# Self loops of the neighbour counts: eight 4-column matmuls a strip in place of four of 392 columns

## The chip, the cores and the metric

The kernel runs as one program on one core of one Trainium2 chip. The metric is device time in microseconds (us); the kernel before takes 3985.91 us, the median of three runs (3983.66 to 3988.76). All lower times are better. The profiles are each of one execution, taken by the hardware profiler.

## The reference, cut to what matters

The network takes 6250 nodes with 128 features and 200,000 edges sorted by destination, runs one graph attention layer (10 heads of 13 features) and then four graph convolutions with self loops. In short:

```python
ft = (hn @ W_att).reshape(n, 10, 13)
scores = einsum('ehd,ehd->eh', ft[src], ft[dst]) / sqrt(13)
ex = exp(scores - segment_max(scores, dst)[dst])
agg = segment_sum(ft[src] * (ex / segment_sum(ex, dst)[dst])[:, :, None], dst)
...                                   # elu, projection, feed-forward on the nodes
# each of the four convolutions, with the same edges:
s = concatenate([src, arange(n)]); d = concatenate([dst, arange(n)])   # the self loops
deg = segment_sum(ones, d); dis = rsqrt(deg)
out = segment_sum((x @ W)[s] * (dis[s] * dis[d])[:, None], d) + b
```

A convolution is thus a product with the matrix A + I, whose entry (source, destination) counts edges, plus 1 on the diagonal. The kernel writes this matrix of counts to memory once, in bf16, and the four convolutions read it back as a moving operand.

## The kernel before, in words

The program goes through stages with a barrier between them: `prelude` (0 to 116 us), `attention` (116 to 2107 us), `normalise`, `general_attention`, `node_update`, and `convolutions` (from about 2360 us to the end). The change lies in `attention` alone.

`attention` is written out in full for NG = 196 groups of 1024 edges (GC = 8 columns of 128), and no loop is left in the program. Beside group k's edges, each step k also makes the counts of strip k: 32 destination nodes (SUB) against all sources. These are 6272 sources as 128 partitions by 49 tiles (NT). The strip is cut in four quarters q of two sets (QS = 2) of four destinations (HALF); a quarter is 2 x 196 columns in a PSUM tile `adj_ps`, of which there are two, taken in turn. A column of a quarter is (destination set a, source tile, destination within the set).

For each quarter, VectorE makes one-hot rows of the keys `ohk` (`key_one_hots`, L937), VectorE and ScalarE make the one-hot rows of the source's low part `ohl` (L932, L1030 and L1037), and TensorE adds up their products in `count` (L1133: four matmuls of 196 columns). Ahead of these, the matmul of L1129 puts the self loops in: the stationary operand is a 32 x 128 slice of `own_low`, the moving one a 32 x 392 window of `own`, a tile of zeros with ones at the strip's own source tile. It opens the accumulation (`start=True`) for all 392 columns. ScalarE then copies the quarter out as bf16 (`copy_quarter`, L1082), and after the fourth quarter the strip goes to memory (L1110).

The attention part of a step is a pipeline of lag LAG = 3: POOL gathers the sources' features with eight indirect DMAs a group (L900) into one of six buffers `fts`. TensorE spreads the destinations' features (`ftd_ps`, L1155), VectorE multiplies both and sums to scores (L951, L987, L992), ScalarE takes exponentials (L1061, L1068), VectorE weights the features (`terms`, L974), and TensorE sums them into `agg_ps` (L1189, L1207 to L1213).

The order on each engine is written out by hand in its `body(k)`. What couples the engines: POOL's first gather of group n waits for `terms` of group n - 6, and its fifth for the shift (L1057) of group n - 4. A quarter waits on TensorE for its keys and for ScalarE's copy of the quarter two before. VectorE's `first_products` waits for all eight gathers of its group.

Of the kernel before, what the change touches and what calls it, by code (L numbers as in the profile page):

```python
# [6 lines left out]
BF16 = mybir.dt.bfloat16  # L7
# [6 lines left out]
P = 128  # L14
# [18 lines left out]
SUB = 32  # L33
NS = NP // SUB
HALF = 4
NA = SUB // HALF
NH = NP // HALF
SC = 2
SW = SC * P
STRIP = NT * SUB  # L40
KEYS = NT * HALF
# [31 lines left out]
def gnn_program(nc, t):  # L73
# [16 lines left out]
    with top:  # L90
# [47 lines left out]
        with ExitStack() as lists:  # L138
            g["src_all"] = sb("src_all", [P, NG, GC], I32, lists)
            g["sched"] = sb("sched", [1, NG // UN, 2 * UN], I32, lists)  # L140
            g["key_cols"] = sb("key_cols", [P, NG, NA, SC], F32, lists)
            g["low_cols"] = sb("low_cols", [P, NG, NA, SC], F32, lists)
            g["shared"] = sb("shared", [WD, NG], F32, lists)
            g["spots"] = sb("spots", [5, P], FP16, lists)
            prelude(nc, t, sb, pb, sem, g, ln_batch)
            stage_over()
            attention(nc, t, sb, pb, sem, g)
            stage_over()
# [594 lines left out]
def attention(nc, t, sb, pb, sem, g):  # L743

    ft_tab, row_tab, agg_tab, adj, sched, src_all, shared, ident, ident_bf, spots, key_cols, low_cols = (g[k] for k in (
        "ft_tab", "row_tab", "agg_tab", "adj", "sched", "src_all", "shared", "ident", "ident_bf", "spots", "key_cols",
        "low_cols"))
# [8 lines left out]
    QS = 2  # L756
# [4 lines left out]
    with ExitStack() as c:  # L761
# [13 lines left out]
        terms = sb("terms", [P, 2, GC, WA], F32, c)  # L775
        res = sb("res", [WD, UN, WA], F32, c)
        iota_sb = sb("iota_sb", [P, KEYS + P], F32, c)
        own = sb("own", [SUB, NA, 2 * KEYS], BF16, c)
        own_low = sb("own_low", [SUB, 2 * P - SUB], BF16, c)
        lo_iota = sb("lo_iota", [P, P], FP16, c)  # L780
        ohk = sb("ohk", [P, 2, NA * SC, KEYS], BF16, c)
        ohl = sb("ohl", [P, 2, NA * SC, P], BF16, c)
# [3 lines left out]
        adj_ps = [pb(f"adj_ps{q}", [P, 512], F32, c) for q in range(2)]  # L786
# [7 lines left out]
        own_made = sem("own_made")  # L794
# [39 lines left out]
        def _(sp):  # L834
# [23 lines left out]
            for j in range(NG // UN):  # L858
                _, base = nc.values_load_multi_w_load_instructions(
                    sched[:, j, :], engines=[mybir.EngineType.SP], min_val=0, max_val=NP,  # L860
                    skip_runtime_bounds_check_because="node numbers, at most NP")
                for u in range(UN):
                    n = j * UN + u
                    if u % 2 == 0:
                        if j:
                            sp.wait_ge(close_done, n - UN + 2)
                        sp.dma_start(rows[0:4, u:u + 2, :], row_tab[n:n + 2].rearrange("g r e -> r g e")
                                     ).then_inc(rows_in[u // 2], 16)
                    if n >= UN:
                        sp.wait_ge(ftd_done, 4 * (n - UN) + 4)  # L870
                    sp.dma_start(win[:, u, :], ft_tab[ds(base[u], WD), :].unsqueeze(0).to_broadcast([2, WD, HD])
                                 ).then_inc(win_in[u], 16)
                    if n >= BACK:
                        store(n - BACK, base[UN + u])
                    if n == WEIGHTS_AT:
                        node_weights()
# [28 lines left out]
        def _(dve):  # L905
# [2 lines left out]
            nc.vector.memset(signs[:, 1:2], RS).then_inc(consts, 1)  # L908
            nc.vector.memset(rows[:], 1.0).then_inc(consts, 1)
            nc.vector.memset(fade[:], 1.0).then_inc(consts, 1)  # L910
            nc.vector.memset(own[:], 0.0).then_inc(own_made, 1)
            nc.vector.memset(own_low[:], 0.0).then_inc(own_made, 1)
            nc.vector.memset(hr_3[:], 0.0).then_inc(rest_zero, 1)
            dve.wait_ge(own_made, 2)
            nc.vector.tensor_copy(own[:, :, KEYS:KEYS + HALF], ident_bf[0:SUB, 0:SUB].rearrange("p (a d) -> p a d", d=HALF)
                                  ).then_inc(own_made, 1)
            nc.vector.tensor_copy(own_low[:, P - SUB:P], ident_bf[0:SUB, 0:SUB]).then_inc(own_made, 1)
            for s in range(2):
                nc.vector.memset(terms[:, s, :, WA - 1:WA], 1.0).then_inc(consts, 1)
# [200 lines left out]
        def _(pe):  # L1120
            def count(k, q):

                pe.wait_ge(keys_done, 4 * k.n + q + 1)
                if q * QC <= LD < (q + 1) * QC:
                    pe.wait_ge(ohl_done, k.n + 1)
                if q >= 2 or k.after(1):
                    pe.wait_ge(strip_done, 4 * k.n + q - 1)
                tile_of = own[:, q * QS:(q + 1) * QS, KEYS - HALF * k.j:2 * KEYS - HALF * k.j]
                nc.tensor.matmul(adj_ps[q % 2][:, 0:QS * KEYS], own_low[:, P - SUB - SUB * k.u:2 * P - SUB - SUB * k.u], tile_of, start=True, stop=False)  # L1129
                for a in range(QS):  # L1130
                    for m in range(SC):
                        n = q * QC + a * SC + m
                        last = nc.tensor.matmul(adj_ps[q % 2][:, a * KEYS:(a + 1) * KEYS], ohl[:, k.s, n, :],  # L1133
                                                ohk[:, k.s, n, :], start=False, stop=(a == QS - 1 and m == SC - 1))
                last.then_inc(adj_done, 1)

            def nearness(k):

                pe.wait_ge(rows_in[k.u // 2], 16 * (k.j + 1))
                if k.after(1):  # L1140
                    pe.wait_ge(oh_done, k.n)
                nc.tensor.matmul(near_ps[:], spots[:], rows[:, k.u, :], start=True, stop=True).then_inc(near_done, 1)
# [73 lines left out]
            def body(k):  # L1216
                nxt, one, two, late = k.at(1), k.at(-1), k.at(-2), k.at(-LAG)
                if late.exists():
                    broadcast_highest(late)
                if two.exists():  # L1220
                    turn_highest(two)
                if k.exists():
                    count(k, 0)
                if nxt.exists():
                    nearness(nxt)
                if k.exists():
                    count(k, 1)
                    count(k, 2)
                if one.exists():
                    last_features(one)  # L1230
                if nxt.exists():
                    closeness(nxt)
                if k.exists():
                    count(k, 3)
                if late.exists():
                    first_sums(late)
                    later_sums(late)
                if k.exists():
                    first_features(k)
                if late.exists():  # L1240
                    if late.after(1):
                        carried(late)
                    last_sum(late)
            zero = Group(0)
            pe.wait_ge(own_made, 4)
            nearness(zero)
            closeness(zero)
            steps(body, LAG)
# [1044 lines left out]
```

## Time and profile before

| | |
|---|---|
| median of 3 runs | 3985.91 us (3983.66 to 3988.76) |
| span of the profiled execution, first to last instruction | 3987.6 us |
| attention stage, first gather to last sum copied out | 117.3 to 2103.9 us |
| convolutions | about 2360 to 3987 us |
| busy over the span | PE 92%, PEld 54%, DVE 54%, ACT 47%, POOL 38% |

No own time apart from the span is given for the profiled execution; the span is taken for it, and it is 1.7 us above the median, inside the spread of the three runs. PE is TensorE's matmuls and PEld its weight loads, which overlap them; DVE is VectorE, ACT ScalarE, POOL GpSimd. Busy time is the time with an instruction recorded; for POOL's indirect DMAs that is the issue alone, and the data land later. The idle time before an instruction is given with what ended it, "issue" being idle time in which the engine waited for nothing that the profile shows. TensorE's clock has two levels here, 1.2 and 2.4 GHz, shown as 0.5 and 1.0; a mean between them is a mixture in time.

### The profile page before, as it was taken

How to read it: one execution, taken by the hardware profiler on the slowest of the kernel's cores; microseconds unless marked ns; L12 is line 12 of the kernel's file. 1: busy time of each engine (PE TensorE's matmuls, PEld its weight loads, DVE VectorE, ACT ScalarE, POOL GpSimd, SP SyncE). 2: the span in 40 equal slices, each digit the busy share in tenths (PEclk: the TensorE clock that was granted, in tenths of full speed). 3: DMA queues.
4: the chain of work that ended last, by engine and by line, in shares of the span. 5: the costliest groups of instructions: out<-in, count | busy, mean ns of one | idle time of the engine just before them, and what ended most of it. 6: DMA issues, size and time to landing. Idle time of an engine off the chain costs nothing. (4 is left out here: it accounts for less than half of the span.)

```text
span 3987.6 us, 61840 instructions
## 1 busy us (share of the span) xinstructions
PE 3679.6 (92%) x21902; PEld 2157.9 (54%) x21902; DVE 2167.3 (54%) x3396; ACT 1880.8 (47%) x5147; POOL 1505.2 (38%) x1605
## 2 busy tenths in 40 slices
PE   5899999999999999999985879999999999999999
PEld 3566666666666666666653544445444544454444
DVE  8788888888888888888874750002100210012000
ACT  4788888888888888888863660002000100011000
POOL 2677777777777777777760000000000000000000
PEclk8788888888888888888886989999999999999999
DMA  6443333333333333333334126665666566665665
GB/s 202 128 109 104 105 106 105 105 106 105 106 105 105 106 106 106 105 106 105 105 92 88 38 65 204 204 196 181 199 194 208 174 194 203 205 189 184 213 204 159
DMA packets 467250, 560.45 MB, mean 141 GB/s; under 512 B 45449, under 2 KB 411684, under 8 KB 466686
## 3 DMA queue, kind: packets, MB, share of 16 engines
q1 hardware_dynamic: 383558, 366.63, 30.4%
q0 software_dynamic: 51168, 107.68, 12.2%
q10 hardware_dynamic: 32248, 82.62, 5.6%
q8 instruction: 155, 2.54, 0.3%
q14 instruction: 121, 0.99, 0.1%
HBM read 455.16 MB, written 103.20 MB: 140 GB/s over the span
## 5 line engine op out<-in xcount | busy, mean ns | idle before, releaser
L900 POOL DMA_INDIRECT fts<-ft_tab,src_all x1568 | 1483.0, 946 | 478.0 <-issue 477.4
L2171 PE MATMUL cv_acc<-cv_cnt,cv_parts 128*128 128x512 bf16 (+1 forms) x7056 | 1431.3, 366 | 0.0
L2171 PEld LDWEIGHTS cv_acc<-cv_cnt,cv_parts 128*128 128x128 bf16 x7056 | 666.0, 98 | 761.7
L2006 DVE TENSOR_TENSOR cv_y<-cv_acc,dis_row 128x512 f32<-128x512 f32 (+1 forms) x52 | 34.4, 661 | 1355.1 <-PE cv_acc L2171 1326.5
L937 DVE TENSOR_TENSOR ohk<-iota_ps,key_cols 128x784 bf16<-128x784 f32 x784 | 724.9, 966 | 6.1
L1030 ACT ACTIVATE dist_l<-lo_iota,low 128x128 bf16<-128x128 f16 x1960 | 593.7, 388 | 18.6 <-ACT low L1025 0.8
L1189 PE MATMUL agg_ps<-terms,oh 128*64 128x141 f32 x2744 | 528.7, 364 | 25.6 <-DVE terms L974 25.0
L1189 PEld LDWEIGHTS agg_ps<-terms,oh 128*64 128x64 f32 x2744 | 458.1, 180 | 80.6 <-DVE terms L974 67.3
L1082 ACT CAST strip<-adj_ps 128x392 bf16<-128x392 f32 x784 | 372.2, 475 | 271.4 <-PE adj_ps L1133 239.2
L1133 PE MATMUL adj_ps<-ohk,ohl 128*128 128x196 bf16 x3136 | 431.2, 263 | 0.0
L951 DVE TENSOR_TENSOR prod<-ftd_ps,fts 128x780 f32<-128x780 f32 (+1 forms) x392 | 271.1, 692 | 220.5 <-DMA fts<-ft_tab,src_all 212.3
L1155 PE MATMUL ftd_ps<-win,ohdT 64*128 64x130 f32 x3136 | 316.5, 326 | 52.2 <-DVE prod L951 51.2
L2140 ACT ACTIVATE cv_sd<-cv_mv,eps 128x1 f32<-128x1 f32 x2 | 0.6, 294 | 739.5 <-DVE cv_tmp L2095 739.5
L1129 PE MATMUL adj_ps<-own,own_low 32*128 32x392 bf16 x784 | 270.7, 345 | 74.3 <-DVE ohk L937 42.1
L1133 PEld LDWEIGHTS adj_ps<-ohk,ohl 128*128 128x128 bf16 x3136 | 235.7, 101 | 180.1 <-issue 178.1
L1155 PEld LDWEIGHTS ftd_ps<-win,ohdT 64*128 64x128 f32 x3136 | 236.1, 212 | 141.4 <-DVE prod L951 75.3
L1037 ACT ACTIVATE ohl<-dist_l 128x1280 bf16<-128x1280 bf16 x196 | 248.9, 1270 | 18.4 <-ACT dist_l L1030 0.7
L974 DVE TENSOR_TENSOR terms<-fts,most_ps 128x1040 f32<-128x1040 f32 x196 | 240.8, 1229 | 9.9 <-ACT most_ps L1061 9.0
L987 DVE TENSOR_REDUCE score<-prod 128x80 f32<-128x1040 f32 x196 | 242.3, 1236 | 6.7
L932 DVE TENSOR_TENSOR ohl<-iota_ps,low_cols 128x768 bf16<-128x768 f32 x196 | 185.7, 948 | 0.0
L1129 PEld LDWEIGHTS adj_ps<-own,own_low 32*128 32x128 bf16 x784 | 72.2, 92 | 205.8 <-issue 115.8
L2124 ACT ACTIVATE cv_stage<-hT 128x896 f32<-128x896 f32 (+2 forms) x8 | 6.7, 852 | 368.9 <-DVEq L169 368.9
(261 smaller groups left out, 2919.9 us busy)
## 6 DMA issues: line engine op xcount, KB each, us to landing
cv_cnt<-adj SPq DMA_DIRECT2D x96, 2048.0 KB, 8.3
cv_cnt<-adj SPq DMA_DIRECT2D x48, 2176.0 KB, 8.6
adj<-strip ACTq DMA_DIRECT2D x196, 392.0 KB
fts<-ft_tab,src_all POOLq DMA_INDIRECT x1568
win<-ft_tab SPq DMA_DIRECT2D x196, 65.0 KB
agg_tab<-res SPq DMA_DIRECT2D x196, 35.2 KB
cv_cnt<-adj SPq DMA_DIRECT2D x8, 512.0 KB, 3.7
agg_tab<-zero_f SPq DMA_DIRECT2D x10, 352.5 KB
```

The source lines that it names most:

```text
L900: nc.gpsimd.indirect_dma_start(fts[u][:, k, :], None, ft_tab[:, :], bass.IndirectOffsetOnAxis(src_all[:, n, k:k + 1], 0)).then_inc(gathere ...
L937: nc.vector.tensor_tensor(ohk[:, k.s, at, :], key_no.unsqueeze(1).to_broadcast([P, QC, KEYS]), columns(key_cols, k)[:, at].unsqueeze(2).to ...
L951: nc.vector.tensor_tensor(by_half(prod[:]), ftd_ps[:, :, 0:n * HD].rearrange("p a (c f) -> p a c f", f=HD), by_half(fts[k.f][:]), ALU.mult ...
L987: nc.vector.tensor_reduce(score[:, k.c, 0:GC * H], prod[:].rearrange("p c (h d) -> p (c h) d", d=DH), AX.X, ALU.add).then_inc(score_done, 1)
L1030: last = nc.scalar.activation(dist_l[:, n, :], lo_iota[:], ACT.Abs, bias=low[:, k.s, n:n + 1], scale=-1.0)
L1037: nc.scalar.activation(ohl[:, k.s, LD:NA * SC, :], dist_l[:], ACT.Relu, bias=1.0, scale=-1.0).then_inc(ohl_done, 1)
L1082: nc.scalar.copy(strip[:, k.s, :, QS * q:QS * (q + 1), :].rearrange("p t a d -> p a t d"), adj_ps[q % 2][:, 0:QS * KEYS].rearrange("p (a t ...
L1129: nc.tensor.matmul(adj_ps[q % 2][:, 0:QS * KEYS], own_low[:, P - SUB - SUB * k.u:2 * P - SUB - SUB * k.u], tile_of, start=True, stop=False)
L1133: last = nc.tensor.matmul(adj_ps[q % 2][:, a * KEYS:(a + 1) * KEYS], ohl[:, k.s, n, :], ohk[:, k.s, n, :], start=False, stop=(a == QS - 1 ...
L1155: last = nc.tensor.matmul(ftd_ps[:, half, m * HD:(m + 1) * HD], ohdT[at, k.u, (c0 + m) * P:(c0 + m + 1) * P], win[at, k.u, :], start=True, ...
L1189: nc.tensor.matmul(agg_ps[0:WD, 0:WA], oh[:, k.o, col, half, :], terms[:, k.s, n, :], start=(n == 0), stop=False)
L2171: last = nc.tensor.matmul(a[:, 0:width], parts[:, r, b, :], cnt[q][:, 0:width // SUB, (b - b0) * SUB:(b - b0 + 1) * SUB], start=(b == 0 an ...
```

## The change

The wide tile `own` goes, with its memset and the copy into it. The two sets of a quarter each open their own accumulation with their first edge matmul (`start=(m == 0)`), and end with a matmul of 4 columns: the same 32 x 128 slice of `own_low` as stationary operand, and four columns of the identity as moving one, added at the four columns that belong to the strip's own source tile (`t0`).

```diff
-        own = sb("own", [SUB, NA, 2 * KEYS], BF16, c)
...
-            nc.vector.memset(own[:], 0.0).then_inc(own_made, 1)
             nc.vector.memset(own_low[:], 0.0).then_inc(own_made, 1)
             nc.vector.memset(hr_3[:], 0.0).then_inc(rest_zero, 1)
-            dve.wait_ge(own_made, 2)
-            nc.vector.tensor_copy(own[:, :, KEYS:KEYS + HALF], ident_bf[0:SUB, 0:SUB].rearrange("p (a d) -> p a d", d=HALF)
-                                  ).then_inc(own_made, 1)
+            dve.wait_ge(own_made, 1)
             nc.vector.tensor_copy(own_low[:, P - SUB:P], ident_bf[0:SUB, 0:SUB]).then_inc(own_made, 1)
...
-                tile_of = own[:, q * QS:(q + 1) * QS, KEYS - HALF * k.j:2 * KEYS - HALF * k.j]
-                nc.tensor.matmul(adj_ps[q % 2][:, 0:QS * KEYS], own_low[:, P - SUB - SUB * k.u:2 * P - SUB - SUB * k.u], tile_of, start=True, stop=False)
+                own_rows = own_low[:, P - SUB - SUB * k.u:2 * P - SUB - SUB * k.u]
                 for a in range(QS):
                     for m in range(SC):
                         n = q * QC + a * SC + m
-                        last = nc.tensor.matmul(adj_ps[q % 2][:, a * KEYS:(a + 1) * KEYS], ohl[:, k.s, n, :],
-                                                ohk[:, k.s, n, :], start=False, stop=(a == QS - 1 and m == SC - 1))
+                        nc.tensor.matmul(adj_ps[q % 2][:, a * KEYS:(a + 1) * KEYS], ohl[:, k.s, n, :],
+                                         ohk[:, k.s, n, :], start=(m == 0), stop=False)
+                    d0, t0 = (q * QS + a) * HALF, a * KEYS + k.j * HALF
+                    last = nc.tensor.matmul(adj_ps[q % 2][:, t0:t0 + HALF], own_rows, ident_bf[0:SUB, d0:d0 + HALF],
+                                            start=False, stop=True)
                 last.then_inc(adj_done, 1)
...
-            pe.wait_ge(own_made, 4)
+            pe.wait_ge(own_made, 2)
```

On TensorE, the stretch from one highest score's turn (L1183 before, L1181 after) to the second quarter of the next strip reads, before:

```order
L1183 MATMUL agg_ps<-ident,score 1x128
L1129 MATMUL adj_ps<-own,own_low 128x392
L1133 MATMUL adj_ps<-ohk,ohl 128x196 x4
L1142 MATMUL near_ps<-rows,spots 128x512
L1129 MATMUL adj_ps<-own,own_low 128x392
L1133 MATMUL adj_ps<-ohk,ohl 128x196 x4
```

and after:

```order
L1181 MATMUL agg_ps<-ident,score 1x128
L1128 MATMUL adj_ps<-ohk,ohl 128x196 x2
L1131 MATMUL adj_ps<-ident_bf,own_low 128x4
L1128 MATMUL adj_ps<-ohk,ohl 128x196 x2
L1131 MATMUL adj_ps<-ident_bf,own_low 128x4
L1140 MATMUL near_ps<-rows,spots 128x512
L1128 MATMUL adj_ps<-ohk,ohl 128x196 x2
L1131 MATMUL adj_ps<-ident_bf,own_low 128x4
L1128 MATMUL adj_ps<-ohk,ohl 128x196 x2
L1131 MATMUL adj_ps<-ident_bf,own_low 128x4
```

Each quarter has one matmul and one weight load more, and what opens it is now an edge matmul; all other work stands where it stood.

On VectorE at the start of the stage, before:

```order
L910 MEMSET fade 64x4
L911 MEMSET own 32x1568
L912 MEMSET own_low 32x112
L913 MEMSET spare 21x896
L915 COPY own<-ident_bf 32x8x4
L917 COPY own_low<-ident_bf 32x32
```

and after:

```order
L909 MEMSET fade 64x4
L910 MEMSET own_low 32x112
L911 MEMSET spare 21x896
L913 COPY own_low<-ident_bf 32x32
```

The memset of `own` and the copy into it are gone, and nothing else moved on that engine.

## Rows read from the trace of the kernel before

**Rows 1.** The page's first part, and TensorE's clock in 40 slices.

```profile
PE 3679.6 (92%) x21902; PEld 2157.9 (54%) x21902; DVE 2167.3 (54%) x3396; ACT 1880.8 (47%) x5147; POOL 1505.2 (38%) x1605
...
PEclk8788888888888888888886989999999999999999
```

**Rows 2.** Busy time by stretch: whole stage, its first 44 us, its middle.

```profile
core 0: us, PE busy (x) PEld busy (x) DVE busy (x) ACT busy (x) POOL busy (x), PEclk, DMA share, GB/s
117.00:2080.00 1963.00, 1809.83 (x12666) 1204.55 (x12666) 1713.77 (x2349) 1584.11 (x4497) 1483.10 (x1569) 0.86 0.40 106
117.00:161.00 44.00, 34.76 (x167) 18.68 (x168) 33.63 (x47) 33.37 (x84) 33.22 (x36) 0.50 0.35 91
...
1000.00:1500.00 500.00, 458.01 (x3251) 305.08 (x3250) 437.35 (x601) 404.38 (x1152) 378.04 (x400) 0.88 0.39 106
```

**Rows 3.** POOL's gathers: durations (ns min/median/max) and starts, idle time before them.

```profile
L900 POOL DMA_INDIRECT fts<-ft_tab,src_all x1568: 941/947/970, 117.3 to 2077.2; - x196
...
  issue: 477.4, 1566
  ACT shift L1057: 0.6, 2
```

**Rows 4.** Waits from 1000 to 1500 us: total us, times, longest us.

```profile
POOL fts L900 <- issue: 121.4, 398, 0.3
...
DVE prod L951 <- DMA fts<-ft_tab,src_all: 55.8, 46, 3.9
...
PE ftd_ps L1155 <- DVE prod L951: 18.0, 20, 2.7
...
PE adj_ps L1129 <- DVE ohk L937: 10.6, 24, 0.5
```

**Rows 5.** Timeline of TensorE (start, us, ...), one group at the full clock.

```profile
1248.67 0.38 PE L1183 MATMUL agg_ps<-ident,score 128*1 128x128 f32 x2
...
1249.92 0.33 PE L1129 MATMUL adj_ps<-own,own_low 32*128 32x392 bf16 x1
1250.18 0.51 PE L1133 MATMUL adj_ps<-ohk,ohl 128*128 128x196 bf16 x4
1250.63 0.34 PE L1129 MATMUL adj_ps<-own,own_low 32*128 32x392 bf16 x1
...
1255.87 0.19 PE L1209 MATMUL agg_ps<-res,move 64*1 64x1 f32 x2
1255.98 0.45 PE L1213 MATMUL agg_ps<-terms,oh 128*64 128x141 f32 x2
1256.37 0.38 PE L1176 MATMUL most_ps<-signs,most 1*128 1x2 f32 x2
1256.68 0.38 PE L1183 MATMUL agg_ps<-ident,score 128*1 128x128 f32 x2
```

**Rows 6.** The same at the half clock, near the stage's start and at its end.

```profile
140.94 0.59 PE L1183 MATMUL agg_ps<-ident,score 128*1 128x128 f32 x2
141.62 0.50 PE L1129 MATMUL adj_ps<-own,own_low 32*128 32x392 bf16 x1
142.06 0.83 PE L1133 MATMUL adj_ps<-ohk,ohl 128*128 128x196 bf16 x4
...
144.43 0.48 PE L1129 MATMUL adj_ps<-own,own_low 32*128 32x392 bf16 x1 [1.00 <-ACT strip L1082]
...
151.28 0.58 PE L1183 MATMUL agg_ps<-ident,score 128*1 128x128 f32 x2
...
2091.58 3.55 PE L1189 MATMUL agg_ps<-terms,oh 128*64 128x141 f32 x14 [1.65 <-DVE terms L974]
...
2096.30 0.58 PE L1176 MATMUL most_ps<-signs,most 1*128 1x2 f32 x2
```

**Rows 7.** Timeline around the last counts and the last gather, all engines.

```profile
2069.91 0.17 ACT L1057 COPY shift<-most_ps 128x2 f32<-128x2 f32 x1
...
2071.88 1.23 DVE L974 TENSOR_TENSOR terms<-fts,most_ps 128x1040 f32<-128x1040 f32 x1
2072.02 0.09 PEld L1129 LDWEIGHTS adj_ps<-own,own_low 32*128 32x128 bf16 x1 [0.86 <-DVE ohk L937]
...
2081.50 0.97 DVE L951 TENSOR_TENSOR prod<-ftd_ps,fts 128x780 f32<-128x780 f32 x1 [6.45 <-DMA fts<-ft_tab,src_all]
```

**Rows 8.** Timeline of VectorE, start of the stage.

```profile
119.04 1.36 DVE L911 MEMSET own<- 32x1568 uint32 x1 [0.28 <-issue]
...
121.39 0.10 DVE L915 COPY own<-ident_bf 32x32 bf16<-32x32 bf16 x1
```

## The prediction

> **What bounds the kernel now.** I read the page's first part and the clock line first, then the stage of the change by windows, then who waits for whom in it, and last single groups in the timeline.
>
> The page makes TensorE look like the bound: PE is busy for 92% of the span and POOL for 38% [rows 1]. That is an average over stages with different limits. The change touches only the attention stage, so that stage is what counts. In it PE is busy 1809.83 of 1963.00 us, VectorE 1713.77, ScalarE 1584.11 and POOL 1483.10 [rows 2]: again PE on top, at 92%. But busy time is not what paces it. POOL's 1568 gathers start from 117.3 to 2077.2 us [rows 3], so one every (2077.2 - 117.3) / 1567 = 1.251 us. The median one takes 0.947 us, and before each stand 0.30 us of idle time that ended with nothing but "issue" (477.4 us over 1566 of them). Over the whole stage all other waits of POOL come to 0.6 us, in two pieces of 0.3 us, the usual gap under another name [rows 3]. So POOL issues gathers back to back from the first to the last, and 8 x 1.251 = 10.0 us is what a group takes.
>
> The others wait for it. From 1000 to 1500 us, fifty groups, VectorE waits 55.8 us for gathered data, and TensorE 18.0 us for VectorE's products, which stand behind that wait [rows 4]. PE has 500.00 - 458.01 = 42 us without a matmul there, 0.84 us a group [rows 2]. Its real reserve is larger, since its busy time stretches with the clock: one whole group at the full clock runs from the turn at 1248.67 to the next at 1256.68 us, 8.01 us without a gap of note [rows 5]. The clock is at its lower level for some of the time (mean 0.86, so (1 - 0.86) / 0.5 = 28% of it [rows 2]); TensorE falls behind there and catches up at the full clock.
>
> The cushion behind POOL can be worked out at the last group, 195. Its gathers start from 2077.2 - 7 x 1.25 = 2068.4 us. The first needs the terms of group 189. The terms at 2071.88 us are those of group 192 [rows 7], so group 189's ended about 2071.88 + 1.23 - 30.0 = 2043.1, 25 us early. The fifth gather (2073.4 us) needs the shift of group 191, about 2069.91 + 0.17 - 10.0 = 2060.1 us, 13 us early. TensorE would have to fall over 13 us further behind before POOL noticed.
>
> **The change, part by part.**
>
> *The matmul that goes.* 784 matmuls of 392 columns. At the full clock one takes 1250.18 - 1249.92 = 0.26 us to the start of the next [rows 5]; at the half clock 142.06 - 141.62 = 0.44 us [rows 6].
>
> *The two that come.* No row shows a 4-column bf16 matmul of 32 rows. The nearest is L1209: one column, 64 rows, f32, which shows as two passes; from its start to the next line's 1255.98 - 1255.87 = 0.11 us, 0.055 us a pass [rows 5]. From above, L1176 with 2 columns and a full 128-column weight load takes 1256.68 - 1256.37 = 0.31 us for two passes, 0.155 each [rows 5]. L1133, full width with a bf16 weight load of 128 columns, takes (1250.63 - 1250.18) / 4 = 0.11 us [rows 5], most of it for 196 columns. So a new one costs 0.055 to 0.155 us, and I take 0.09, nearer to L1133's weight load than to the f32 one. Two are 0.18 us (0.11 to 0.31) against 0.26 at the full clock: a quarter saves 0.08 us (-0.05 to +0.15), a group 0.32 us (-0.2 to +0.6). TensorE's group at the full clock becomes 7.7 us (7.4 to 8.2). At the half clock the removed one is worth 0.44, so a quarter saves 0.13 to 0.33 us.
>
> *The added weight load* is in these numbers. The one that L1129 has shows 0.09 us [rows 7]. The Trainium skill, "TensorE: Matmul & The Clock Gate", LDWEIGHTS (loading the stationary operand), says that a load's time goes by the columns loaded, not by the rows, at columns / 1.2 ns: an estimate of 107 ns for this one, although only 32 rows carry anything, and the change doubles the number of such loads. With 0.107 for each new pair a quarter would save 0.26 - 0.21 = 0.05 us in place of 0.08. This speaks against the change but does not turn it; the row's 0.09 us is a little below the rule.
>
> *What hides all of it.* TensorE's 7.7 us at the full clock stands against POOL's 10.0, as 8.01 did. The cover is POOL's unbroken issue, which neither a quicker nor a slower quarter reaches; without it a group would be worth 0.32 us, 63 us in 196 groups. What is late next after an earlier quarter is nothing new: ScalarE's copies come sooner, `strip` leaves sooner, and VectorE's next keys are queued behind the same wait for gathered data (55.8 us in 50 groups, rows 4). Sum over 196 groups: 0.
>
> *The opening matmul* of a quarter now needs `ohl` and `ohk`, where L1129 needed only constants. The waits in `count` stand ahead of both versions alike, so nothing starts later: 0.
>
> *VectorE's start.* The memset (1.36 us) and the copy (0.10) go [rows 8], with 0.28 us of issue before the memset: TensorE's and VectorE's first work moves up by 1.4 to 1.7 us. POOL started at 117.3 us and waits for none of it: 0 again.
>
> *The end of the stage.* The last quarter's L1129 is at 2072.02 us, and VectorE then waits 6.45 us for the last gathers, until 2081.50 us [rows 7]; what follows has no counts in it: 0. The chain behind, three groups' sums one after another, runs at the half clock: the 14 passes of L1189 and what follows take 2096.30 - 2091.58 = 4.72 us [rows 6], where the full clock takes less. If the clock happened to be up for it, the stage would end some 5 us sooner: three times 3.55 us of L1189 would halve. I leave that out of the sum and put it in the range.
>
> *Later stages* have the same instructions: 0. Sum: the profiled 3987.6 us stays 3987.6, and the median, 1.7 us below it, stays 3985.9. I say 3985.7 for the small lead that the tail may gain.
>
> **The rivals.**
>
> *A. Nothing happens (my forecast).* 3985.7 us, 3981 to 3990 by the spread of the three runs, 5 us, and the clock's phase.
>
> *B. The busiest engine is the bound.* PE is busy 92% of the stage and holds the counts' accumulators, for which ScalarE waits. If TensorE paced the groups, its saving would come through: 0.32 x 196 = 63 us, 3923 us, and up to 0.6 x 196 = 118 us, 3868 us. For it: the 92%. Against it: the 8.01 us group and POOL's gaps, all 0.30 us. The Trainium skill, "Perfetto Trace Analysis", Identifying the Most-Contended Engine, names the engine of highest occupancy as the one to improve (for TensorE it wants the weight loads' share instead of the matmuls'); by that rule the engine here would be VectorE at 87%, and POOL, at 76% busy, would be ranked below it. The trace disagrees: POOL's 0.30 us gaps are part of its issue, so it is full.
>
> *C. Slower: the clock stays down.* TensorE's clock was 0.50 for the stage's first 44 us, in which PE was busy 34.76 us, with gaps [rows 2]; fewer columns make for more gaps. At the half clock a group costs 151.28 - 140.94 = 10.3 us without sums, of which 1.0 idle, and the sums 4.7 [rows 6]: 14.0 us, less 4 x 0.2 for the change: 13.2 us. It decides when the share f of time at the half clock has f / 13.2 + (1 - f) / 7.7 below 1 / 10, that is f over 0.55, a mean clock under 0.72; at f = 0.60 a group takes 10.27 us, 0.27 x 196 = 53 us more: 4039 us. Against it: it corrects itself. At the half clock a full group (13.2 us) exceeds POOL's 10, so TensorE falls behind and its gaps close; it stood at 28%, far from 55%, and the same first 44 us cost POOL nothing. [...]
>
> *D. The tail at the full clock.* 5 us less, 3980.7 us, which is still no change by the bound below. For it: the phase of the clock differs from run to run. Against it: PE stands idle before the tail in both kernels.
>
> **How the numbers follow.** A measurement of this kernel can tell about 0.2%, 8 us, from no change. A has 0.80, D 0.06, B 0.06 and C 0.08. So faster 0.06, no change 0.86, slower 0.08. A and D alone hold 0.86, so the range is A's, widened below to D and above by the unknown start of the clock's phases: 3979 to 3992.
>
> **What would show it.** POOL's gathers should again start every 1.25 us, from about 117 to 2077 us, with idle time by "issue" alone. The new small matmuls should take 0.06 to 0.15 us each to the next start; PE's busy share of the stage should fall by some points while VectorE's wait for gathered data stays or grows. PEclk in the stage may sink below 0.86 without harm, as long as it stays over 0.72. I am wrong if POOL shows waits for `terms` or the shift (C), or if its gathers come closer together than 1.25 us, which B needs and I see no cause for.

## The result and the profile after

The changed kernel takes 3992.27 us (median of 20 runs, 3988.93 to 3994.79), the kernel before 3985.69 us (median of 20, 3982.99 to 3989.68). The ratio is 1.0015, with a 95% interval of 1.0009 to 1.0022: 6.6 us slower, inside the 0.2% that I called no change, but clear of noise, and 0.3 us above the top of my range. The profiled execution spans 3987.1 us. That it is not longer than the 3987.6 of before is the luck of two single executions: this one took 3988.93 us in all, the lowest of the twenty. So the comparison has to be made by stretches.

The attention stage by windows, after (span, then busy us of PE, PEld, VectorE, ScalarE and POOL, then granted clock, DMA share, GB/s):

```profile
117.00:2080.00 1963.00, 1872.64 (x13454) 1253.49 (x13454) 1715.41 (x2350) 1588.38 (x4497) 1480.27 (x1570) 0.84 0.40 106
```

Against [rows 2], TensorE is busy for 63 us more, not less, and its clock is 0.84 instead of 0.86. POOL, after (durations in ns, first and last start, then idle time and what ended it):

```profile
L899 POOL DMA_INDIRECT fts<-ft_tab,src_all x1568: 940/944/971, 117.5 to 2074.0; - x196
...
  issue: 477.3, 1567
  ACT shift L1053: 0.3, 1
```

As in [rows 3], it issues without a gap, one gather every 1956.5 / 1567 = 1.249 us. The stage lost nothing: 1956.5 us of gathers here against 1959.9 in the trace of before. All traces made later of kernels with eight gathers, with the change or without it, show 1956.2 to 1956.4 us, so it is the trace of before that was 3.6 us long.

The time went in the convolutions, whose lines the change does not touch. From the first product `cv_w_ps` to the end of the last `cv_acc`, before and after:

```profile
2357.83:3981.82 1623.99, 1612.74 (x8082) 780.04 (x8083) 200.52 (x306) 108.79 (x261) 0.00 (x0) 1.00 0.62 195
```

```profile
2351.28:3981.30 1630.02, 1614.45 (x8082) 781.32 (x8083) 200.53 (x306) 109.08 (x261) 0.00 (x0) 1.00 0.62 194
```

That is 6.0 us more for the same instructions. From first product to first product (and to the end of the last `cv_acc`) the four layers take 0.2, 1.3, 0.5 and 4.0 us more than before. The time is lost at the starts of layers. TensorE at the start of the fourth layer in the timeline (start, us, line, count, idle before), before:

```profile
3574.78 2.01 PE L2198 MATMUL cv_w_ps<-cv_W,cv_stage 128*128 128x128 f32 x14 [1.52 <-ACT cv_stage L2124]
3577.55 1.80 PE L2198 MATMUL cv_w_ps<-cv_W,cv_stage 128*128 128x128 f32 x14 [0.76 <-issue]
3579.18 1.46 PE L2185 MATMUL cv_acc<-cv_cnt,cv_parts 128*128 128x512 bf16 x6
3580.48 0.85 PE L2198 MATMUL cv_w_ps<-cv_W,cv_stage 128*128 128x128 f32 x6
3581.97 1.16 PE L2198 MATMUL cv_w_ps<-cv_W,cv_stage 128*128 128x128 f32 x8 [0.64 <-issue]
```

and after:

```profile
3570.27 2.01 PE L2196 MATMUL cv_w_ps<-cv_W,cv_stage 128*128 128x128 f32 x14 [1.51 <-ACT cv_stage L2122]
3573.03 1.47 PE L2196 MATMUL cv_w_ps<-cv_W,cv_stage 128*128 128x128 f32 x11 [0.75 <-issue]
3577.49 0.60 PE L2196 MATMUL cv_w_ps<-cv_W,cv_stage 128*128 128x128 f32 x3 [3.00 <-issue]
3577.93 2.13 PE L2183 MATMUL cv_acc<-cv_cnt,cv_parts 128*128 128x512 bf16 x6
```

In both, TensorE stands in the middle of a product, where it waits for no semaphore ("issue"): 0.64 us before, 3.00 us after. Both times it goes on 7.2 us after the layer's first product (3581.97 - 3574.78 = 7.19, 3577.49 - 3570.27 = 7.22); what differs is how many instructions earlier it ran dry. After the long stop six 512-column matmuls take 2.13 us in place of 1.46, since the clock has fallen. The mean granted clock of the 29.8 us from the layer's first product is 1.00 before and 0.94 after:

```profile
3574.70:3604.50 29.80, 28.33 (x169) 18.27 (x170) 19.15 (x26) 22.87 (x57) 0.00 (x0) 1.00 0.71 225
```

```profile
3570.20:3600.00 29.80, 25.98 (x150) 17.73 (x151) 17.76 (x24) 20.61 (x51) 0.00 (x0) 0.94 0.62 196
```

The second layer has a stop of 1.26 us that it did not have before:

```profile
2764.87 0.38 PE L2196 MATMUL cv_w_ps<-cv_W,cv_stage 128*128 128x128 f32 x2 [1.26 <-issue]
```

What is missing is the instructions themselves. The page has two queues that carry instructions, q8 and q14. That q8 is TensorE's shows in its count, which follows TensorE's stream through all runs with eight gathers: 155 packets before and with 16 more instructions, 156 with 32 to 256 more, 162 with the change, while q14 stays at 121 or 122. Before and after:

```profile
q8 instruction: 155, 2.54, 0.3%
```

```profile
q8 instruction: 162, 2.65, 0.3%
```

One packet is 2.54 MB / 155 = 16.4 KB, 256 instructions of 64 bytes. The change adds 1568 instructions to TensorE's stream, 6.1 packets, and the queue shows 7 more. So everything behind the stage stands 1568 - 6 x 256 = 32 instructions further on in its packet.

The attention stage is written out without a jump, but the convolutions have branches and loops, also on TensorE. The trace's records have a branch (the one on `irregular` behind `product(1)`) 0.7 us after the fourth layer's first product. The next packet on q8 starts 4.5 us after the first product before and 4.6 us after, and takes 1.1 to 1.2 us. TensorE goes on 1.6 and 1.5 us after it has landed. That the jump is the reason why this packet comes no earlier is an inference: no run leaves the jump out.

### The profile page after: what moved, and what is told of

Same layout as the page of the kernel before. It is cut to its first block and busy times, and to the rows that moved or that the text cites. A ratio compares the mean times of both kernels' runs of the same rounds, so it can differ in the third digit from the quotient of the medians.

```text
span 3987.1 us, 63406 instructions
## 1 busy us (share of the span) xinstructions
PE 3744.5 (94%) x22686; PEld 2210.2 (55%) x22686; DVE 2166.2 (54%) x3394; ACT 1885.5 (47%) x5147; POOL 1502.3 (38%) x1605
## 5 line engine op out<-in xcount | busy, mean ns | idle before, releaser
L1128 PE MATMUL adj_ps<-ohk,ohl 128*128 128x196 bf16 x3136 | 568.2, 265 | 51.1 <-DVE ohk L933 26.1
L1187 PE MATMUL agg_ps<-terms,oh 128*64 128x141 f32 x2744 | 562.4, 380 | 16.6 <-DVE terms L970 13.8
L1187 PEld LDWEIGHTS agg_ps<-terms,oh 128*64 128x64 f32 x2744 | 489.5, 191 | 35.3 <-DVE terms L970 21.8
L1131 PEld LDWEIGHTS adj_ps<-ident_bf,own_low 32*128 32x128 bf16 x1568 | 143.6, 92 | 284.2 <-issue 284.2
L1128 PEld LDWEIGHTS adj_ps<-ohk,ohl 128*128 128x128 bf16 x3136 | 183.9, 98 | 192.3 <-issue 110.0
L1131 PE MATMUL adj_ps<-ident_bf,own_low 32*128 32x4 bf16 x1568 | 272.8, 174 | 0.0
```

The lines of the kernel that those rows point to most:

```text
L1131: last = nc.tensor.matmul(adj_ps[q % 2][:, t0:t0 + HALF], own_rows, ident_bf[0:SUB, d0:d0 + HALF], start=False, stop=True)
L1187: nc.tensor.matmul(agg_ps[0:WD, 0:WA], oh[:, k.o, col, half, :], terms[:, k.s, n, :], start=(n == 0), stop=False)
```

## The experiments

**The place in the packet.** Theory F: the 6.6 us are this shift and nothing else. The rivals: the small matmuls or the clock cost the time in the attention stage (P), or the 6 us are scatter between two executions (S). I put idle semaphore increments into TensorE's stream in the attention stage, spread over its 196 steps. (The expectations of e1 and e4 count the convolutions from another point, 1618 us before and 1624 us after; by the stretch used here these are 1623.99 and 1630.02, the same 6 us apart.)

```diff
+        PADS = 224          # 32, 256, 128, 16, 64 in the kernel before
...
                     last_sum(late)
+                if k.exists():
+                    for _ in range(PADS * (k.n + 1) // NG - PADS * k.n // NG):
+                        pe.sem_inc(padding, 1)
```

> The changed kernel with 224 idle semaphore increments spread over the 196 steps of TensorE in the attention stage. The change itself added 1568 instructions to TensorE's stream (784 matmuls, 784 weight loads); the trace shows that stream fetched in packets of 16384 bytes, 256 instructions of 64 bytes, so all code behind the stage stands 1568 mod 256 = 32 instructions further in its packet. 1568 + 224 = 1792 = 7 x 256 puts it back. Theory F (fetch: the 6.6 us are lost in the convolutions, where TensorE waits for the packet behind a jump): convolutions 1618 us as in the kernel before (1624 in the changed one), median 3985.7 +- 2. Rival P (the small matmuls or the clock cost the time in the attention stage or at its end): nothing comes back, median 3992 or a little more. Rival S (one trace against one trace: the 6 us of the convolutions are scatter): convolutions anywhere, the median stays 3992.

Measured: 3986.06 us (11 runs), ratio to before 1.0001 (0.9992 to 1.0010). The convolutions take 1624.95 us and the stop in the fourth layer is 0.70 us.

> The kernel before with 32 idle semaphore increments on TensorE in the attention stage, so that the code behind it stands at the place in its packet that it has in the changed kernel, and nothing else is changed. Theory F: as slow as the changed kernel, about 3992 us, with 3 us of idle TensorE in the second product of the last layer and 1.5 us at the start of the second layer. Rivals P and S: 3985.7 us as before.

Measured: 3991.17 us (11 runs), ratio 1.0014 (1.0005 to 1.0023). The convolutions take 1630.22 us. The fourth layer's start shows the stop of the changed kernel at the same instruction:

```profile
3570.02 2.01 PE L2203 MATMUL cv_w_ps<-cv_W,cv_stage 128*128 128x128 f32 x14 [1.52 <-ACT cv_stage L2129]
3572.79 1.46 PE L2203 MATMUL cv_w_ps<-cv_W,cv_stage 128*128 128x128 f32 x11 [0.76 <-issue]
3577.25 1.01 PE L2203 MATMUL cv_w_ps<-cv_W,cv_stage 128*128 128x128 f32 x3 [3.00 <-issue]
```

> Control: the kernel before with 256 idle increments, one whole packet. The place of the later code in its packet is that of the kernel before. Theory F: 3985.7 us. A theory by which more instructions on TensorE cost time wherever they stand: slower, by up to 256 x 0.05 = 13 us.

Measured: 3985.99 us (11 runs), ratio 0.9997 (0.9988 to 1.0006), convolutions 1623.97 us. The increments themselves cost nothing here.

> The kernel before with 128 idle increments, half a packet. Theory F: the later code's stalls are at other places, so that the convolutions take another time than 1618 us, either way by some us (3980 to 3995); P and S: 3985.7 us.

Measured: 3986.68 us (11 runs), ratio 0.9999 (0.9990 to 1.0008). The convolutions take 1623.49 us, the shortest of all, with no stop in the fourth layer; the total gains nothing that can be measured.

> The kernel before with 16 idle increments, half the shift of the changed kernel. In the last layer's start TensorE comes to the end of its packet 6.5 us after its first product in the kernel before and stands until 7.2 us; in the changed kernel it comes there after 4.2 us and stands from there until 7.2 us, 3 us idle. Theory F: the next packet is there at 7.2 us whatever the place, so with 16 instructions the idle time is between, 1.5 to 2.6 us, and the convolutions take 1625 to 1629 us (1624.0 before, 1630.0 changed, from the first product to the last accumulation). Rival T (a threshold other than the place in the packet): 1624.0 or 1630.0.

Measured, one run: 3985.40 us, convolutions 1625.02 us. The stop is 1.75 us and stands in the first accumulation, between the places of the two others:

```profile
3573.35 1.03 PE L2190 MATMUL cv_acc<-cv_cnt,cv_parts 128*128 128x512 bf16 x4
3576.12 0.59 PE L2190 MATMUL cv_acc<-cv_cnt,cv_parts 128*128 128x512 bf16 x2 [1.75 <-issue]
```

> The kernel before with 64 idle increments, twice the shift of the changed kernel. Theory F: the end of the packet lies before or at the jump to the layer's second part, so the next packet is asked for earlier or the wait falls into time in which TensorE waits for ScalarE and VectorE anyway: no 3 us stall inside the last layer's second product, convolutions 1623 to 1627 us. Rival T (more instructions past a point cost time steadily): 1630 us or more.

Measured, one run: 3987.47 us, convolutions 1628.79 us, a miss. The stop is not gone; it has moved up to the jump and merged with the one there (the branch itself is recorded with 5.79 us in place of 0.34):

```profile
3568.30 2.01 PE L2203 MATMUL cv_w_ps<-cv_W,cv_stage 128*128 128x128 f32 x14 [1.52 <-ACT cv_stage L2129]
3574.96 3.05 PE L2203 MATMUL cv_w_ps<-cv_W,cv_stage 128*128 128x128 f32 x14 [4.65 <-issue]
```

Together, with all times read from the timelines:

| shift in the packet, kernel | stop in layer 4, us | goes on, us after the layer's first product | convolutions, us |
|---|---|---|---|
| 0, before | 0.64 | 7.19 | 1623.99 |
| 0, before + 256 | 0.59 | 7.14 | 1623.97 |
| 0, changed + 224 | 0.70 | 7.25 | 1624.95 |
| 16, before + 16 | 1.75 | 7.17 | 1625.02 |
| 32, before + 32 | 3.00 | 7.23 | 1630.22 |
| 32, changed | 3.00 | 7.22 | 1630.02 |
| 64, before + 64 | 4.65 | 6.66 | 1628.79 |
| 128, before + 128 | none | | 1623.49 |

TensorE goes on about 7.2 us after the layer's first product, wherever its packet ends, and the stop is what is left until then. The records of q8 bear this out: the packet starts 4.5 to 4.6 us after the first product in the first six kernels of the table, at 3.9 us with 64, where TensorE also goes on earlier, and with 128 it had started 0.2 us before the first product, so there is no stop. The clock adds to the long stops: over 29.8 us from the layer's first product its mean is 1.00 with the stop of 1.75 us, 0.94 and 0.89 with those of 3.00 us (changed, and before + 32) and 0.94 with that of 4.65 us.

That settles F: the same shift without the change costs 5.1 us, the change without the shift 0.4 us or nothing, and P and S fall. The six-gather kernels further down, whose TensorE streams are those of before or as long as that of the changed kernel, repeat it in five more traces: convolutions of 1624.05 and 1623.98 us with a stop of 0.70 and 0.60 us (e8, e11), and of 1630.00, 1629.96 and 1630.34 us with a stop of 3.00 us (e9, e10, e12).

The changed kernel at shift 0 keeps 1.0 us more in the convolutions than before (e5, below, 1.2), mostly in the first and third layers (407.17 and 404.34 against 406.88 and 403.79 us from first product to first product). VectorE's stream has also lost two instructions. No run was made for this, but e12, whose TensorE stream is as long as the changed kernel's and whose VectorE stream is that of before, has 406.93 and 403.96 us there, which points to VectorE's stream.

**The small matmuls.** The traces show that my sum for TensorE was wrong too. One group at the full clock, after:

```profile
1006.68 0.38 PE L1181 MATMUL agg_ps<-ident,score 128*1 128x128 f32 x2
...
1007.99 0.34 PE L1128 MATMUL adj_ps<-ohk,ohl 128*128 128x196 bf16 x2
1008.27 0.17 PE L1131 MATMUL adj_ps<-ident_bf,own_low 32*128 32x4 bf16 x1
1008.37 0.34 PE L1128 MATMUL adj_ps<-ohk,ohl 128*128 128x196 bf16 x2
1008.65 0.17 PE L1131 MATMUL adj_ps<-ident_bf,own_low 32*128 32x4 bf16 x1
1008.76 0.34 PE L1128 MATMUL adj_ps<-ohk,ohl 128*128 128x196 bf16 x2
```

A quarter takes 1008.76 - 1007.99 = 0.77 us where [rows 5] have 1250.63 - 1249.92 = 0.71, and of the groups that lie wholly at the full clock the shortest takes 8.10 us (of 66) in place of 8.00 (of 89). The small matmul itself is followed after 0.10 us, as I had it. But between the second edge matmul's start and the small one's there are 0.18 us, where an edge matmul follows an edge matmul after 0.09. Each change from 128 rows to 32 and back costs some 0.1 us, and before each weight load of the small matmuls TensorE's loader idles, as the waits of the stage say (total us, times, longest us):

```profile
PEld adj_ps L1131 <- issue: 284.2, 1568, 0.3
```

The test is to leave everything and take the small matmuls over 128 rows, of which 96 are zero:

```diff
-        own_low = sb("own_low", [SUB, 2 * P - SUB], BF16, c)
+        own_low = sb("own_low", [P, 2 * P - SUB], BF16, c)
...
-            nc.vector.tensor_copy(own_low[:, P - SUB:P], ident_bf[0:SUB, 0:SUB]).then_inc(own_made, 1)
+            nc.vector.tensor_copy(own_low[0:SUB, P - SUB:P], ident_bf[0:SUB, 0:SUB]).then_inc(own_made, 1)
...
-                    last = nc.tensor.matmul(adj_ps[q % 2][:, t0:t0 + HALF], own_rows, ident_bf[0:SUB, d0:d0 + HALF],
+                    last = nc.tensor.matmul(adj_ps[q % 2][:, t0:t0 + HALF], own_rows, ident_bf[:, d0:d0 + HALF],
```

> The changed kernel with the 224 idle increments, and the 4-column matmuls taken over 128 rows instead of 32: own_low gets 128 rows, of which those from 32 on are zero, and the moving operand is all of the identity's rows. In the traces a quarter takes 0.76 us in the changed kernel (four edge matmuls and two of 4 columns) against 0.71 before, since the step from a 128-row matmul to a 32-row one takes 0.18 us and the step back 0.105, where one 128-row matmul follows another after 0.09. Theory R (a change between 32 and 128 rows keeps the next weight load from being made ahead): without it a small matmul costs 0.05 to 0.09, a quarter 0.45 to 0.55 us and a group at the full clock 7.1 to 7.4 us in place of 8.1. Rival N (a matmul of few columns costs its 0.17 us of latency whatever its rows): 8.1 us a group as in the changed kernel. In both the whole kernel stays at 3986 us, since GpSimd's gathers pace the stage at 10.0 us a group; if TensorE paced it, R would give 0.8 x 196 = 157 us.

Measured: 3986.39 us (11 runs), ratio 1.0005 (0.9996 to 1.0014). One quarter in the timeline, and the matmul behind it:

```profile
1006.92 0.34 PE L1130 MATMUL adj_ps<-ohk,ohl 128*128 128x196 bf16 x2
1007.10 0.16 PE L1133 MATMUL adj_ps<-ident_bf,own_low 128*128 128x4 bf16 x1
1007.13 0.33 PE L1130 MATMUL adj_ps<-ohk,ohl 128*128 128x196 bf16 x2
1007.30 0.17 PE L1133 MATMUL adj_ps<-ident_bf,own_low 128*128 128x4 bf16 x1
1007.40 0.38 PE L1142 MATMUL near_ps<-rows,spots 5*128 5x512 f16 x1
```

The small matmul now starts 0.09 us after the edge matmul and is followed after 0.03 us, so a quarter is 1007.40 - 1006.92 = 0.48 us, inside my 0.45 to 0.55. Its record still says 0.17 us: the latency is there, but it is not in the way. And the loader's idle time before the small matmuls, 284.2 us in the changed kernel, is gone: the view of this line lists none before its 1568 weight loads. A group at the full clock has TensorE busy for 7.21 us (median of 63), inside my 7.1 to 7.4; the shortest takes 7.53 us from turn to turn, as TensorE now waits for ScalarE or VectorE in each. Theory R holds, N falls. PE's busy time in the stage is 131 us below before's:

```profile
117.00:2080.00 1963.00, 1678.26 (x13450) 1277.63 (x13450) 1713.04 (x2351) 1582.91 (x4497) 1480.32 (x1571) 0.84 0.40 106
```

And the kernel is no faster for it, which is what POOL as the pace demands. The Trainium skill has the rule that I did not weigh: "TensorEngine Tiling (Array Packing)", Key Properties, says that changing the tiling mode drains TensorE. The trace agrees, with about 0.1 us for each change, though it does not show what happens inside TensorE in that time.

**Without POOL's cover.** Whether the gathers hide all of this can be seen by leaving two of eight out, with the part of the attention that needs them:

```diff
-                for k in range(GC):
+                for k in range(GC if n < FU else 6):
...
-                dve.wait_ge(gathered[k.f], 16 * GC * (k.n // FU + 1))
+                dve.wait_ge(gathered[k.f], 16 * GC + 16 * 6 * (k.n // FU))
```

> The kernel before with six gathers a group in place of eight from the seventh group on; the two columns that are not gathered keep their old features, so that part of the attention is left out. GpSimd's pace becomes 7.5 us a group, under TensorE's 8.0 at the full clock and VectorE's 8.75 us of work. The cover theory: the stage then shows what TensorE and VectorE take by themselves, 8.8 to 9.3 us a group, the gathers from first to last 1725 to 1820 us. If something else than the gathers paced the stage, it stays near 1956 us.

> The changed kernel with six gathers a group, the same part left out. The group at the full clock is 8.10 us against 8.00 before, so without the cover the change costs: 0 (if VectorE paces) to 0.1 us a group at the full clock, and it may gain at the half clock, where the removed matmul took 0.44 us: between -20 and +20 us against the kernel before with six gathers. By the recorded prediction's sum it would save 0.32 a group, 63 us.

> The changed kernel with 128-row small matmuls and six gathers a group, the same part left out. Theory R with TensorE as the pace: 0.8 us a group less than the changed one with six gathers, down to VectorE's 8.75 us, which then paces: 1715 to 1740 us. Rival N: as the changed one with six gathers.

Then two more, to part the change of rows from the number of columns:

```diff
 # e11: the kernel before, six gathers, 392 columns over 128 rows
+        own = sb("own", [P, NA, 2 * KEYS], BF16, c)
+        own_low = sb("own_low", [P, 2 * P - SUB], BF16, c)
...
 # e12: the changed kernel, six gathers, 196 columns in place of 4
+                    last = nc.tensor.matmul(adj_ps[q % 2][:, a * KEYS:(a + 1) * KEYS], own_rows,
+                                            own[:, q * QS + a, KEYS - HALF * k.j:2 * KEYS - HALF * k.j],
```

> The kernel before with six gathers a group (the same part left out), and its 392-column matmul taken over 128 rows instead of 32 (own and own_low with 128 rows, zero from 32 on). With six gathers the gathers ran 1770 us in the kernel before (mean clock 0.94 from 200 to 1700 us), 1871 in the changed one (0.86), 1787 with 128-row small matmuls (0.87). Theory H (both the step between 32 and 128 rows and the clock, which falls when fewer columns are streamed): as many columns as before and no step, so a group at the full clock takes 0.1 x 8 = 0.6 to 0.8 us less than 8.0, VectorE paces at 8.75: 1740 to 1775 us, the clock 0.9 or above. Rival I (idle time alone brings the clock down): more idle TensorE at that pace, clock 0.87 or lower, 1775 us or more.

> The changed kernel with six gathers a group (the same part left out), and its small matmuls widened from 4 to 196 columns: one for each set, over 32 rows, from the tile own as before. Instructions, order and steps between 32 and 128 rows are those of the changed kernel; only columns are added, 8 x 192 a group, 0.64 us at the full clock. Theory H (the columns streamed keep the clock up): the clock comes back above 0.90 and the stage is faster than the changed one in spite of more work, 1770 to 1830 us of gathers against 1871. Rival S (the steps and the instructions cost the 100 us): as slow or slower, 1871 to 2000 us.

Measured, one run each; gathers from the first start to the last:

| kernel, six gathers | gathers, us | TensorE busy in a group at the full clock, median, us | clock, 200 to 1700 us |
|---|---|---|---|
| before (e8) | 1770.2 | 8.21 | 0.94 |
| changed (e9) | 1870.8 | 8.11 | 0.86 |
| changed, small matmuls over 128 rows (e10) | 1786.9 | 7.14 | 0.87 |
| before, 392 columns over 128 rows (e11) | 1733.9 | 7.80 | 0.97 |
| changed, 196 columns (e12) | 1989.7 | 8.72 | 0.84 |

The stage follows TensorE and VectorE once POOL has time: POOL then waits for them (e8, 1000 to 1500 us):

```profile
POOL fts L900 <- ACT shift L1057: 103.2, 56, 3.5
```

So the cover was real. Without it the change would have cost 100 us, five times the worst that I expected, and against the 63 us gained of the prediction's sum. These are single executions, but the whole times are as far apart, 3913.15 and 3806.86 us: 106 us, of which 6 are the convolutions'. The longer group at the full clock, 0.10 us (8.10 against 8.00, shortest to shortest; the table's medians of busy time stand the other way round), explains at most 0.1 x 196 = 20 us. The rest goes with the clock; 200 to 1700 us, before and changed with six gathers:

```profile
200.00:1700.00 1500.00, 1432.18 (x10761) 943.77 (x10761) 1440.92 (x1988) 1334.34 (x3809) 940.47 (x998) 0.94 0.36 102
```

```profile
200.00:1700.00 1500.00, 1468.37 (x10795) 989.15 (x10792) 1373.16 (x1877) 1265.72 (x3594) 886.78 (x941) 0.86 0.34 96
```

Two pairs differ in the changes of rows alone: the kernel before gains 36 us without them (e8 to e11), the changed one 84 us (e9 to e10). e10 missed its 1715 to 1740 us all the same, by 47 us, at a clock of 0.87; e11 came out just under its 1740 us, at 0.97, against rival I. My theory H said that the streamed columns also hold the clock up, and that e12 would win some back. It lost another 119 us, at 0.84, inside the range of rival S, though TensorE was recorded busy almost without a gap:

```profile
200.00:1700.00 1500.00, 1499.38 (x10159) 953.86 (x10159) 1314.96 (x1768) 1195.00 (x3388) 836.13 (x885) 0.84 0.33 90
```

In that form H is wrong. Still, e10 has less work than e11 (7.14 against 7.80 us a group), neither changes rows within a count, and e10 is 53 us slower at a lower clock, which S does not explain either. What exactly moves the clock stays open.

## Why the prediction was wrong

**The step that failed** is "*Later stages* have the same instructions: 0". Their instructions are the same but stand 32 further in their packet, and this costs 6.0 us in the trace (1.3 of them in the second layer, 4.0 in the fourth), 5.1 to 6.6 in the medians. It was within reach: the page had the instruction queue, the trace of before already showed stops of 0.64 to 0.76 us with no waited semaphore behind the layers' jumps, and I counted the added instructions without asking what they push.

**What bounds the stage**: right. POOL issued every 1.25 us, its waits stayed at 0.3 us in total, and e1 and e5 show the change worth nothing at shift 0, whether TensorE has more or less to do.

**The removed matmul against the two that came**: wrong in sign at the full clock. I had 0.08 us saved a quarter (-0.05 to +0.15); it is about 0.06 us lost where the neighbours are edge matmuls, just past the far end. The two small matmuls cost 0.10 us each to the next start, as priced. What I left out is the change of rows ahead of each, 0.18 us where an edge matmul follows after 0.09. The quarter before had one such step, into L1129, and it stood unnoticed in my price for L1133: the 0.45 us over four starts are three of 0.09 and one of 0.18. The changed quarter has two. A whole group lost 0.10 us, not 0.24, since the fourth quarter follows `near_ps` sooner (0.35 us after its start, 1009.94 to 1010.29, against 0.46 before, 1251.77 to 1252.23). So 8.10 us lies within my 7.4 to 8.2, in spite of the wrong sign. At the half clock the change did save, though less than the 0.13 to 0.33 us that I gave a quarter: 1.08 us (143.25 to 144.33) against 1.18 (144.43 to 145.61).

**Rival B**, the busiest engine as the bound: fell, with PE at 95% of the stage and no cost. **Rival C**, the lower clock: the clock did sink, from 0.86 to 0.84, and POOL never noticed, well above the 0.72 from which I said it decides. Its first half is real where the cover is gone (e9), and the correction that I trusted is weaker than I thought: TensorE was busy for 1468.37 of 1500 us there, the gaps closed, and the clock was still at 0.86. **Rival D**, the tail: 23.9 us from the last gather to the last sum against 26.7 us, in a trace whose kernel is slower all the same. The traces of the kernel before with idle increments have 24.0 to 26.2 us there, so this is scatter and not the change. VectorE's start and the end of the stage cost nothing, as said. TensorE's busy share rose instead of falling.

**The chances.** Slower by 0.15% lies in "no change" by my bound, to which I gave 0.86. But I drew 3979 to 3992 only from mechanisms inside the changed stage, and that the time fell only 0.3 us outside is luck: the same shift by another number of instructions would have cost nothing (e4) or 1 us (e6).

## What to carry to other kernels

A change in the number of instructions on an engine moves all code behind it, and where that code jumps, as here, it can shift stops of several microseconds that belong to no line. Before a difference of a few microseconds is put down to a change, run it once with idle instructions that bring the later code back to its place. And a small matmul is cheap only in the row shape of its neighbours: over all 128 rows, zeros included, it adds 0.03 us where over 32 it adds 0.19.

## What the runs showed of the hardware that I had not expected

- A 4-column matmul between 196-column ones of 128 rows costs 0.18 + 0.10 us from start to start if it is over 32 rows, 0.09 + 0.03 if it is over 128, where two edge matmuls are 0.09 apart: 0.19 us added against 0.03.
- A packet of 256 instructions for TensorE started 4.5 to 4.6 us after the fourth layer's first product and TensorE went on at 7.1 to 7.3 us, in 12 of the 13 kernels that wait for it; in the thirteenth (e7) it was 3.9 and 6.7 us. With a stop of 3.0 us the mean granted clock of the 29.8 us from that first product was 0.94 (the changed kernel) and 0.89 (e2), without it 1.00.
- A stage with less work for TensorE can run at a lower clock and be slower: 1786.9 us of gathers at 0.87 with 7.14 us of TensorE's work a group (e10), 1733.9 us at 0.97 with 7.80 (e11). And the clock was at 0.84 with TensorE recorded busy for 1499.38 of 1500 us (e12). The cause is open.
